# The norm factors of the routing rounds: nine VectorE operations in place of a GpSimd power, and the result stores without a loop

## The reference, cut to what matters

```python
x = x + layernorm(attn(layernorm(x)))       # "norm 1" inside, "norm 2" outside
x = x + layernorm(ffn(layernorm(x)))        # "norm 3" inside, "norm 4" outside

# layernorm: (x - mean) / sqrt(var + 1e-5), over the 128 channels
# attn: dots = (x P) M (x P)^T per head; (dots (x P)) mixed by mixer_w, plus mixer_b
# ffn, for each of the 4096 tokens:
logits = xt @ gate_w.T                      # 8 experts
idx    = top_k(logits + beta, 2)
c      = sigmoid(logits at idx)
out    = sum over the 2 of c * (silu(xt Wg[e]) * (xt Wu[e])) Wd[e]  +  the shared expert
```

## Time and profile before

| | us |
|---|---|
| median of 3 runs | 298.35 |
| lowest and highest run | 295.73, 310.52 |
| span of the profiled execution | 262.8 |
| median less span | 35.55 |
| busy: TensorE / VectorE / GpSimd / ScalarE | 229.9 / 146.0 / 169.9 / 112.1 |

### The profile page before, as it was taken

The page is one execution under the profiler, slowest core; times in us unless marked ns, Lnnn a source line. Parts: engine busy times, 40 slices in busy tenths (PEclk is TensorE's granted clock), DMA queues, the critical chain, the costliest instruction groups (busy, mean ns, idle before and its releaser), DMA issues.

```text
span 262.8 us, 5844 instructions
## 1 busy us (share of the span) xinstructions
PE 229.9 (87%) x1466; PEld 178.0 (68%) x1466; DVE 146.0 (56%) x657; ACT 112.1 (43%) x423; POOL 169.9 (65%) x216
## 2 busy tenths in 40 slices
PE   8977885969998849998998999998999989988980
PEld 2855773444453425445997999998999978978340
DVE  3976775637575946677443544443544434521595
ACT  2957581361656511654333343343334333310771
POOL 7965548785878787777774666665665755760530
PEclk9999595685999975999999999999999999999997
DMA  6796001110111111298648868878687578404973
GB/s 169 219 341 167 0 21 56 38 54 31 51 44 41 54 41 51 90 297 295 200 141 266 292 211 288 283 231 277 216 277 260 176 251 277 151 23 172 393 273 120
DMA packets 38538, 44.95 MB, mean 171 GB/s; under 512 B 8150, under 2 KB 23395, under 8 KB 38512
## 3 DMA queue, kind: packets, MB, share of 16 engines
q1 hardware_dynamic: 32672, 34.00, 40.0%
q0 software_dynamic: 4320, 8.53, 10.1%
q10 hardware_dynamic: 1520, 2.10, 2.2%
HBM read 14.77 MB, written 11.68 MB: 101 GB/s over the span
## 4 chain that ended last, share of the span: by engine, by line
SPq 34%; PE 22%; issue 14%; POOL 10%; DVE 9%; DMA 6%; ACT 3%; POOLq 1%; ACTq 0%; DVEq 0%
SPq L393 13%; SPq L390 11%; PE bank L1167 5%; POOL expert_rows L520 5%; PE bank L1064 3%; SPq L396 3%; POOL rstd L512 3%; PE bank L1048 3%; POOL expert_results L539 2%; DMA xnT<-expert_results 2%; PE bank L1140 2%; SPq L397 2%; PE bank L1101 2%; DVE X L1035 2%; ACT work L597 2%
## 5 line engine op out<-in xcount | busy, mean ns | idle before, releaser
L539 POOL DMA_INDIRECT expert_results<-eo,rowt x71 | 69.4, 978 | 38.6 <-issue 28.6
L520 POOL DMA_INDIRECT expert_rows<-src,slot x64 | 62.3, 973 | 24.6 <-issue 17.3
L1234 PE MATMUL bank<-xTr,wcur 128*128 128x128 f32 x568 | 75.0, 275 | 0.0
L1234 PEld LDWEIGHTS bank<-xTr,wcur 128*128 128x128 f32 x568 | 69.2, 192 | 0.5 <-issue 0.5
L993 DVE TENSOR_TENSOR work<-work,bank 128x256 f32<-128x256 f32 x71 | 29.8, 421 | 54.7 <-ACT work L694 49.9
L694 ACT ACTIVATE work<-bank 128x256 f32<-128x256 f32 x71 | 27.2, 384 | 66.9 <-PE bank L1234 66.9
L1249 PE MATMUL bank<-down,work 128*128 x284 | 44.3, 279 | 1.8 <-DVE work L993 1.7
L1249 PEld LDWEIGHTS bank<-down,work 128*128 128x128 f32 x284 | 37.3, 192 | 3.4 <-issue 2.7
L1167 PE MATMUL bank<-xT,gu_f 128*128 128x512 f32 x64 | 36.0, 700 | 0.0
L999 DVE TENSOR_SCALAR eo<-bank,rowt 128x128 f32<-128x128 f32 x71 | 24.6, 346 | 5.9 <-PE bank L1249 5.8
L1215 PE MATMUL bank<-ident,rowt 128*128 128x128 f32 x71 | 19.6, 278 | 3.8 <-DMA wcur<-gu_f 3.7
(11 more groups left out here) (177 smaller groups left out, 329.0 us busy)
## 6 DMA issues: line engine op xcount, KB each, us to landing
wcur<-gu_f SPq DMA_DIRECT2D x71, 256.0 KB
rowt<-expert_rows SPq DMA_DIRECT2D x71, 66.0 KB
X<-n_L_attn_in_sequence_bwc SPq DMA_DIRECT2D x8, 256.0 KB, 4.0
X<-expert_results SPq DMA_DIRECT2D x8, 256.0 KB, 6.7
xnT<-expert_results ACTq DMA_DIRECT2D x8, 256.0 KB, 7.2
out<-X SPq DMA_DIRECT2D x7, 256.0 KB, 2.5
expert_results<-eo,rowt POOLq DMA_INDIRECT x71, 2.7
gu_f<-in_L_ffn_gate_proj_w SPq DMA_DIRECT2D x1, 1024.0 KB, 7.2
```

The costliest lines, as they stand in the source:

```text
L520: nc.gpsimd.indirect_dma_start(rows_d, bass.IndirectOffsetOnAxis(ap=slot[i % SRC][:, n // TOPK, n % TOPK:n % TOPK + 1], axis=0), src[i % S ...
L539: nc.gpsimd.indirect_dma_start(res_d, bass.IndirectOffsetOnAxis(ap=rowt[v][:, P:P + 1].bitcast(U32), axis=0), eo[v][:], None, bounds_check ...
L1234: last = mm(gu_ps[v % 3][:, n * P:(n + 1) * P], wcur[v][:, n * P:(n + 1) * P], xTr[v % 4][:], start=True, stop=True)
```

## The change

`powers` goes from GpSimd. VectorE gets `factors(u, lo, hi)`: a first guess for y = v to the power -0.5 from v's bits (multiply the bits by -0.5 and add a constant, as numbers), then a first step with tuned constants, then a second step of higher order; nine operations on [128, 1 or 2, 4] numbers, each with a semaphore increment and a wait on it (`factor_c`). It is called after the variances that it takes. The waits on `rstd2_done` and `rstd3_done` go. On GpSimd the stores are written out for all 71 slots instead of a loop, without the `sem_inc` on `waits_apart`. The powers of norms 1 and 4 stay.

```diff
@@ -138,6 +138,8 @@
 
         vpe = [sb(f"vpe_{u}", [P, 2, G]) for u in range(2)]
         rstd = [sb(f"rstd_{u}", [P, 2, G]) for u in range(2)]
+        seed = [sb(f"seed_{u}", [P, 2, G]) for u in range(2)]
+        ratio = [sb(f"ratio_{u}", [P, 2, G]) for u in range(2)]
         st3 = [sb(f"st3_{u}", [P, G, 6]) for u in range(2)]
         mv3 = [sb(f"mv3_{u}", [P, G, 2]) for u in range(2)]
         src = [sb(f"src{u}", [P, TOPK, G, ROW]) for u in range(SRC)]
@@ -265,8 +267,7 @@
         vpe2_done = sem("vpe2_done")
 
 
-        rstd3_done = sem("rstd3_done")
-        rstd2_done = sem("rstd2_done")
+        factor_c = sem("factor_c")
         x1_done = sem("x1_done")
         st3_w = sem("st3_w")
         mv3_done = sem("mv3_done")
@@ -325,7 +326,6 @@
         sum_done = sem("sum_done")
         out_sent = sem("out_sent")
 
-        waits_apart = sem("waits_apart")
         block = ctx.enter_context(nc.Block())
 
         def after(eng, s, value):
@@ -500,48 +500,26 @@
             nc.gpsimd.memset(empty_row[:, P:P + 1].bitcast(I32), NOWHERE).then_inc(route_consts, 1)
             ln1(QS + 1)
 
-            def powers(i, lo=0, hi=2):
-
-                u = i % 2
-                if lo == 0:
-                    gp.wait_ge(vpe3_done, i + 1)
-                    after(gp, xt_done, (i - 1) * G)
-                if hi == 2:
-                    gp.wait_ge(vpe2_done, i + 2)
-                    after(gp, x1_done, i * G)
-                ins = nc.gpsimd.tensor_tensor(rstd[u][:, lo:hi, :], vpe[u][:, lo:hi, :], mhalf[:, lo:hi, :], ALU.pow)
-                if lo == 0:
-                    ins.then_inc(rstd3_done, 1)
-                else:
-                    ins.then_inc(rstd2_done, 1)
-
             def scatter(i):
                 for n in range(G * TOPK):
                     nc.gpsimd.indirect_dma_start(
                         rows_d, bass.IndirectOffsetOnAxis(ap=slot[i % SRC][:, n // TOPK, n % TOPK:n % TOPK + 1], axis=0),
                         src[i % SRC][:, n % TOPK, n // TOPK, :], None).then_inc(rows_out[i % SRC], 16)
 
-            powers(-1, lo=1)
             ln1(QS + 2)
-            powers(0, hi=1)
-            powers(0, lo=1)
             ln1(QS + 3)
             for i in range(STEPS):
-                if i + 1 < STEPS:
-                    powers(i + 1, hi=2 if i + 2 < STEPS else 1)
                 gp.wait_ge(src_x_done, i + 1)
                 gp.wait_ge(src_done, i + 1)
                 scatter(i)
 
-            def store(j, v):
-                gp.wait_ge(eo_done, j * UNROLL + v + 1)
-                gp.sem_inc(waits_apart, 1)
+            for r in range(SLOTS):
+                v = r % UNROLL
+                gp.wait_ge(eo_done, r + 1)
                 nc.gpsimd.indirect_dma_start(
                     res_d, bass.IndirectOffsetOnAxis(ap=rowt[v][:, P:P + 1].bitcast(U32), axis=0),
                     eo[v][:], None, bounds_check=TOPK * T - 1, oob_is_err=False
                 ).then_inc(res_out[v], 16)
-
-            slots(store, 0, gp)
 
             for n, (s, at, count) in enumerate(units[:ROOT]):
                 u = n % 2
@@ -767,23 +745,33 @@
             stats1(6)
             stats1(7)
 
-            def second_power(i):
-
-                if i < 2:
-                    dve.wait_ge(rstd2_done, i + 1)
-                else:
-                    dve.wait_ge(rstd3_done, i)
+            factored = [0]
+
+            def factors(u, lo, hi):
+                v, y, t, r = (f[u][:, lo:hi, :] for f in (vpe, rstd, seed, ratio))
+
+                def link(ins):
+                    factored[0] += 1
+                    ins.then_inc(factor_c, 1)
+                    dve.wait_ge(factor_c, factored[0])
+
+                link(nc.vector.tensor_scalar(y.bitcast(I32), v.bitcast(I32), -0.5, float(0x5F1FFFF9), ALU.mult, ALU.add))
+                link(nc.vector.tensor_tensor(t, y, y, ALU.mult))
+                link(nc.vector.scalar_tensor_tensor(out=t, in0=t, scalar=-0.703952253, in1=v, op0=ALU.mult, op1=ALU.mult))
+                link(nc.vector.scalar_tensor_tensor(out=y, in0=t, scalar=1.68191391, in1=y, op0=ALU.add, op1=ALU.mult))
+                link(nc.vector.tensor_tensor(t, y, y, ALU.mult))
+                link(nc.vector.tensor_tensor(t, t, v, ALU.mult))
+                link(nc.vector.tensor_scalar(r, t, 0.375, -1.25, ALU.mult, ALU.add))
+                link(nc.vector.tensor_tensor(r, r, t, ALU.mult))
+                link(nc.vector.scalar_tensor_tensor(out=y, in0=r, scalar=1.875, in1=y, op0=ALU.add, op1=ALU.mult))
 
             def variance2(i):
                 dve.wait_ge(sumsq_done, i + 1)
-                if i >= 2:
-                    second_power(i - 2)
                 nc.vector.tensor_scalar(vpe[(i - 1) % 2][:, 1, :], sumsq[i % 2][:], 1.0 / P, EPS, ALU.mult,
                                         ALU.add).then_inc(vpe2_done, 1)
 
             def residual(i):
 
-                second_power(i)
                 for n in range(G):
                     nc.vector.scalar_tensor_tensor(
                         out=tile(x1, i, n), in0=attn_ps[i][:, n * P:(n + 1) * P],
@@ -797,11 +785,9 @@
                     last = nc.vector.bn_aggr(mv3[i % 2][:, n, :], st3[i % 2][:, n, :])
                 last.then_inc(mv3_done, 1)
                 dve.wait_ge(mv3_done, i + 1)
-                after(dve, rstd3_done, i - 1)
                 nc.vector.tensor_scalar(vpe[i % 2][:, 0, :], mv3[i % 2][:, :, 1], EPS, None, ALU.add).then_inc(vpe3_done, 1)
 
             def normalise(i):
-                dve.wait_ge(rstd3_done, i + 1)
                 after(dve, rows_out[i % SRC], i // SRC * SENT)
                 for n in range(G):
                     nc.vector.tensor_scalar(src[i % SRC][:, 0, n, 0:P], tile(x1, i, n), mv3[i % 2][:, n, 0:1],
@@ -943,12 +929,20 @@
                                             ALU.min).then_inc(expert_table, 1)
 
             variance2(0)
+            dve.wait_ge(vpe2_done, 1)
+            factors(1, 1, 2)
             residual(0)
             variance2(1)
+            dve.wait_ge(vpe3_done, 1)
+            dve.wait_ge(vpe2_done, 2)
+            factors(0, 0, 2)
             xnT_copy(4)
             normalise(0)
             residual(1)
             variance2(2)
+            dve.wait_ge(vpe3_done, 2)
+            dve.wait_ge(vpe2_done, 3)
+            factors(1, 0, 2)
             dve.wait_ge(router_w_in, 32)
             dve.wait_ge(route_consts, 1)
             choose(0)
@@ -962,6 +956,10 @@
                     hidden(i - 2, 0)
                 if i + 2 < STEPS:
                     variance2(i + 2)
+                    dve.wait_ge(vpe2_done, i + 3)
+                if i + 1 < STEPS:
+                    dve.wait_ge(vpe3_done, i + 2)
+                    factors((i + 1) % 2, 0, 2 if i + 2 < STEPS else 1)
                 if i == 1:
                     xnT_copy(6)
                 choose(i)
```

## The result

The changed kernel took 312.73 us (median of 4 runs, 307.58 to 317.25) beside 301.01 us for the kernel before (295.73 to 310.52): ratio 1.040, 95% interval 1.030 to 1.051. It is slower, and the forecast of 299.0 us with no change is wrong.

The account below looks back on a forecast made before the run. It took the slot loads' wait for VectorE's `row_i` as the bound, with GpSimd pacing rounds 5 to 7. Net +0.25 us plus 0.35 for round 0's clock turned 298.35 into 299.0 us; 8-in-10 range 294.5 to 304.

Parts of the forecast that it names:

- Bound and place: SP's slot loads wait for VectorE's `row_i` at the end of `early_rows`, round 6; everything behind moves with it.
- Cost of one call: Each `factors` call on VectorE: nine links of about 0.20 us, 1.80 us for four columns, 1.85 for eight.
- Round 0: VectorE's two calls at the start: marks at 23.27, 28.2 and 33.6 us, choose(0) 3.2 us late, TensorE 2.6 late.
- term of 0.35 us for round 0's clock: Added for TensorE regaining full clock later after longer waits between 26 and 35 us; bounds nothing and 2.86 us.
- Rounds 1 to 5: `factors` before each choose delays the mask 0.45 us a round, 1.05 in round 1; choose(5) at 92.4 us.
- The 0.45 us a round: In rounds 1 to 5, the part of each call before choose that the gap until the logits doesn't hide.
- net +0.25 us: At `early_rows` in round 6: powers off the path, factors on it, so SP starts 0.25 us later.
- The sum: Whole kernel: +0.25 and +0.35 us, span 262.8 to 263.4, time 298.35 to 299.0 us.
- 35.55 us: The median run's excess over the profile's span, left unchanged in the forecast.
- The clock stays low: Rival: TensorE at low clock in rounds 3 to 5, +9.2 us, 307.5 us; chance 0.12.
- The saving reaches the end: Rival: rounds 1 and 2 meet TensorE's full clock, -5.1 us, 293.2 us; chance 0.08.
- Cheaper links: Rival: 0.16 us a link in `factors`, -3.6 us, 295.4 us; chance 0.18 shared with dearer links.

Follow-up runs that it names:

- after_fourth: The changed kernel unaltered, measured again on a 264 us chip: 266.58 us, ratio 0.996 to the kernel before.
- after_third: The changed kernel unaltered, on a 264 us chip: 267.15 us, ratio 1.010 to the kernel before.

## Why the prediction was wrong, step by step

- *Bound and place.* Right: SyncE follows `row_i`, and behind it nothing changed (189.5 against 187.9 us to the end). The powers had been the bound of rounds 5 to 7; they went.
- *Cost of one call.* Right: 0.20 us a link, 1.79 us for four columns; vpe to choose 2.02, forecast 2.05. Links hardly got dearer beside the scatters: with GpSimd issuing (91.13 to 92.95 us) nine took 1.82 us, the 0.20 of the quiet Newton chain, and the dearest of the nine calls in that profile, in round 6, cost 0.28 us more. So what the Trainium skill's "GPSIMD Engine Reference", "Key points", says of shared SBUF interfaces bore a small price here at most.
- *Round 0.* Right within 0.15 us at each of the three marks in the profile above; in the seven others choose(0) came up to 1.8 us later than forecast. That is more than the whole term of 0.35 us for round 0's clock, and the clock rows further up differ from execution to execution by more than it.
- *Rounds 1 to 5.* Right on a 264 chip: normalise(6) 97.47 for a forecast of 96.8, choose(6) 103.47 for 102.7, the last `row_i` 108.09 for 107.4, scatters ending at 128.3 for 127.9. In `after_fourth` the table ended 2.8 us sooner, so luck with the clock is part of such a match. What the text named only as 9.10 + 0.45 a round has a plainer name: VectorE had become the bound.
- *The 0.45 us a round on the timed chip, and the power as pure cost.* This is the step that failed: the net +0.25 us at the table was carried over to a chip on which it doesn't hold. There the table moved by 13 to 19 us (108.2 to 121.5 and 127.6), of which 9.3 and 11.6 came between choose(1) and choose(6) (62.6 us to 71.9 and 74.2), at the same chain lengths as on the other sort (60.8 us to 57.7 and 54.8). The prediction had no term for late handoffs, and it took the wait of 3.46 us for the factor as waste that a free VectorE would use. Of VectorE's waits up to the table on 301 chips, 6.1 us are remote in the kernel before (6.8 with its stores written out), 9.5, 11.5 and 11.3 with nine operations, 18.0 with four. In the kernel before, other waits are shorter by as much than on the 264 chip (for the power 7.4 instead of 8.6, for the input of vpe 4.7 + 0.7 = 5.4 instead of 7.5, for the logits 3.2 instead of 5.9). That fits late handoffs falling into time in which it waited anyway; no run tests it.
- *The sum.* The base was wrong as well: I read 35.55 us as lying outside the span and moved on. It is 1.8 us; the rest is the other sort of chip, and it was the one thing in the data which said that the profile's rows need not hold for the timed runs. A gap of 12% between a profile and its own runs should have widened the range, on both sides.
- *The rivals.* "The clock stays low" is real but small: 5.4 us between two runs of the same kernel. It struck between 16 and 70 us, not in rounds 3 to 5 as the rival had it, where the rows read full clock on 264 chips, and kernels without the change meet it too. The Trainium skill's "TensorE: Matmul & The Clock Gate", "A second HAM failure mode", has a clock that oscillates with frequent short idle times. The first 70 us of those rows agree with it; what follows doesn't (TensorE busy 9.12 of 10 us at granted clock 1.00). "The saving reaches the end": not with nine operations; with four 0.4 to 2.7%, in the quickest runs mostly by the rival's own reason, more of the full clock in the early rounds. "Cheaper links": no.
- *Stores written out.* I took nothing; measured 0.992 [0.986, 0.998] on a 264 chip and 297.09 beside 302.5 us on a 301 chip. By its medians it is the one version that beat both kernels on both sorts of chip, by no more than the runs spread. That the stores' idle time is "mostly before their data" was a misreading that did no harm: of 38.6 us in the earlier trace rows 28.6 are "issue", and writing the stores out left 27.7 in `after_third`.

**What stays open.** That the late handoffs in the rounds on a 301 chip go with GpSimd's indirect stores is shown, by taking those of the rounds away, in one profile. What in the chip makes them late isn't, nor whether the semaphore or the waiting engine's own next instruction is held up: SyncE's loads without a semaphore speak for more than semaphores. Nor is it shown why the kernel before, with the same 64 scatters, has a third of the remote waits of the one with four operations: that the power gives a pause of 1.67 us after each eight scatters, or that its slower rounds put fewer handoffs beside them, is argued only; scatters with an empty pause between them weren't tried. How much of the changed kernel's loss is TensorE's clock falling behind such waits (0.67 and 0.50 from 100 to 120 us in the first profile) isn't divided either. Of the 34.9 us between the spans of the kernel before on both chips 34.0 lie in the slot stage behind the table (189.5 against 155.5 us), where GpSimd's stores run as well, and no run took these away.

## What to carry to other kernels

Compare a profile's span with the times of its own kernel first: if they differ by more than a few us, the profile was taken under other conditions, and no estimate built on it holds within that gap. Work moved off a slow engine onto a path must be counted in the new bound's busy share: here nine links of 0.20 us took VectorE to 94% of a round, four left TensorE the bound and gained 0.4 to 2.7%. Before a gain is put down to the operations that were cut, lay the clock rows of the two profiles side by side: here 5.4 of 8.4 us were the clock. And a wait may be a cushion: where handoffs came late, the kernel with idle time on VectorE lost less than the tighter ones, though why isn't shown.

## What the runs showed of the hardware that I had not expected

- One kernel, unaltered, takes 263.6 to 264.7 us on two chips and 301.1 to 302.5 us on two others.
- On the latter, handoffs among TensorE, ScalarE and VectorE, and from VectorE to itself, come up to 4.7 us after the work that the trace shows as done, beside GpSimd's indirect stores or within 3.1 us of the start of the last of eight, and SyncE's loads without a semaphore come up to 3.5 us apart, where most are 0.5 to 0.8 us apart. With the rounds' stores as plain DMAs of SyncE the rounds have no such waits, and the table ends at 107.1 us instead of 121.5 to 127.6.
- In runs of one kernel on one chip TensorE's granted clock can take different courses from 16 us on, with and without the change. The two furthest apart (0.91 and 0.50 from 20 to 38 us) end the table of the same kernel 5.4 us apart.
